# Row maximum of causal attention on TensorE: one head per bank and step, against three heads in three banks per burst on 32-row groups

## What is computed

```
q = (h @ Wq.T) as 16 heads of 32;  k = h @ Wk.T;  v = h @ Wv.T   (one key and value head for all 16)
q, k = rmsnorm(rope(q)), rmsnorm(rope(k))
scores = q k^T * 32**-0.5, causal
attn = softmax(scores);  out = attn @ v
x = x + ga * (rmsnorm(out) @ Wo.T)
then: layer norm, router (8 of 64 experts), experts and a shared MLP, x = x + gb * ffn
```

## Time and profile before

| | us |
|---|---|
| median of three runs | 1232.77 (1232.52 to 1236.47) |
| span of the profiled execution | 1233.0 |
| PE busy in it (matmul) | 1168.1 (95%) |
| VectorE busy | 972.6 (79%) |
| ScalarE busy | 762.0 (62%) |
| row maximum matmuls (L1092), 384 | 146.7 |
| row maximum reductions (L1610), 304 | 191.3 |

### The profile page before, as it was taken

How to read it: one execution, slowest core, us unless ns; L and a number is a source line. 1 busy time by engine, 2 the same in 40 slices (tenths; PEclk the granted TensorE clock), 3 DMA queues, 4 the chain that set the end, 5 groups by cost and what they waited for, 6 DMA issues and landing times.

```text
span 1233.0 us, 25541 instructions
## 1 busy us (share of the span) xinstructions
PE 1168.1 (95%) x8905; PEld 879.7 (71%) x8905; DVE 972.6 (79%) x1881; ACT 762.0 (62%) x1507; POOL 497.9 (40%) x375
## 2 busy tenths in 40 slices
PE   8988999999999988999999999999999999999996
PEld 4455556555565655555557899999999999999982
DVE  4678776756657888775767889899888999999976
ACT  3456555555664644455564477787777887777841
POOL 1122212102122111201100148887888778788740
PEclk9999999989999998999999999999999999999999
DMA  9570000000000000003004179999999999999988
GB/s 349 172 302 1 2 18 2 10 9 2 15 10 10 9 1 22 1 10 95 29 14 141 25 225 299 289 302 302 292 295 306 299 297 296 298 301 294 298 231 290
DMA packets 75167, 189.95 MB, mean 154 GB/s; under 512 B 11544, under 2 KB 12184, under 8 KB 74832
## 3 DMA queue, kind: packets, MB, share of 16 engines
q1 hardware_dynamic: 44704, 116.27, 28.0%
q0 software_dynamic: 28672, 71.32, 23.5%
q10 hardware_dynamic: 1712, 1.32, 0.3%
HBM read 136.36 MB, written 52.51 MB: 153 GB/s over the span
## 4 chain that ended last, share of the span: by engine, by line
PE 71%; DVE 13%; DVEq 4%; issue 3%; DMA 3%; ACT 3%; POOL 0%; SPq 0%; POOLq 0%; ACTq 0%
PE ps L1328 22%; PE ps L1367 12%; PE ps L1147 8%; PE ps L1314 5%; PE ps L1177 4%; PE ps L1132 4%; PE ps L1060 4%; PE ps L1092 4%; DVE nmax L1610 3%; PE ps L1117 2%; DMA acc_dram<-y,slots 1%; PE ps L1032 1%; PE ps L1164 1%; DMA wq<-in_wq_t 1%; PE ps L1195 1%
## 5 line engine op out<-in xcount | busy, mean ns | idle before, releaser
L730 POOL DMA_INDIRECT acc_dram<-y,slots x128 | 252.2, 1971 | 74.1 <-issue 47.9
L1610 DVE TENSOR_REDUCE nmax<-ps 128x1 f32<-128x512 f32 (+3 forms) x304 | 191.3, 656 | 95.3 <-PE ps L1096 52.4
L839 ACT ACTIVATE probs<-ps 128x512 f32<-128x512 f32 (+1 forms) x320 | 159.0, 554 | 87.2 <-PE ps L1132 86.3
L681 POOL TENSOR_SCALAR_AFFINE_SELECT probs<-probs 128x512 f32<-128x512 f32 x64 | 44.3, 691 | 376.7 <-ACT probs L839 376.6
L715 POOL DMA_INDIRECT xg<-h_dram,slots x128 | 130.7, 1021 | 84.4 <-DVE slots L1801 40.5
L1092 PE MATMUL ps<-kpad,qpT 128*128 128x512 f32 (+3 forms) x384 | 146.7, 450 | 15.5 <-DVE nmax L1610 13.4
L1328 PE MATMUL ps<-x_hi,e_gu_hi 128*112 128x256 f32 (+1 forms) x768 | 120.1, 278 | 0.0
L1132 PE MATMUL ps<-qT,kT 98*128 98x512 f32 (+1 forms) x320 | 115.1, 437 | 5.0 <-ACT probs L839 4.8
L1328 PE MATMUL ps<-x_hi,e_gu_lo 128*112 128x256 f32 (+1 forms) x768 | 119.6, 278 | 0.0
L1812 DVE TENSOR_TENSOR e_gu_lo<-e_gu,e_gu_hi 128x1408 fp32r<-128x1408 f32 x64 | 103.8, 1622 | 11.0 <-ACT e_gu_hi L960 9.9
L1328 PE MATMUL ps<-x_lo,e_gu_hi 128*112 128x256 f32 (+1 forms) x768 | 109.9, 279 | 0.0
(11 more groups left out here) (238 smaller groups left out, 2375.1 us busy)
## 6 DMA issues: line engine op xcount, KB each, us to landing
e_gu<-in_gate_up SPq DMA_DIRECT2D x64, 704.0 KB, 7.3
e_d<-in_w_down SPq DMA_DIRECT2D x64, 224.0 KB, 4.7
acc_dram<-h SPq DMA_DIRECT2D x2, 4608.0 KB, 26.0
e_d<-in_w_down SPq DMA_DIRECT2D x64, 128.0 KB, 5.4
wmod_b<-in_wmod SPq DMA_DIRECT2D x2, 2048.0 KB, 22.0
xg<-h_dram SPq DMA_DIRECT2D x16, 256.0 KB, 7.0
acc_a<-acc_dram SPq DMA_DIRECT2D x8, 512.0 KB, 10.0
acc_b<-acc_dram SPq DMA_DIRECT2D x8, 512.0 KB, 7.7
```

The lines of the kernel that those rows point to most:

```text
L730: pool.indirect_dma_start(out=acc_dram[a], out_offset=bass.IndirectOffsetOnAxis(ap=slots[:, at:at + 1], axis=0), in_=y[e % 2][:, h, :], in ...
L839: act.activation(probs[:, n % PROBS, 2 * pr:2 * pr + 2, off:CW], unit_bank(2 * n + pr)[:, :, off:CW], ACT.Exp).then_inc(s_exp, 1)
L1610: dve.tensor_reduce(nmax[:, 1 if lo else 0, first:first + heads], max_view(n, heads, hi - lo), AX.X, ALU.max, negate=True).then_inc(s_max, 1)
```

## The change

The keys are stored without zeros: `kq` holds the same 32 rows of keys on all four groups of 32 partitions. For that DVE writes the keys four times side by side (`ks4`), PE transposes them once more to 128 rows, and ACT copies them once. A head's matmul then reads only its own 32 rows of `qpT` and `kq`. The banks of a tile are ordered so that banks next to each other hold heads of different row groups. Up to three banks make a burst: PE issues the matmuls of its banks in turn, one of each bank, then the mask matmuls; DVE takes the maximum over all banks of the burst with one instruction (two where the widths differ). A tile has 2, 3, 6, 6, 7, 8, 11, 11 bursts by its place i, spread over the 16 steps, 108 in all. The three banks are the same as before, so PE waits before each burst until the one before it is reduced. The pass still has 384 matmuls and 176 mask matmuls, and 116 reductions. The memset of `kpad` is gone.

```diff
--- before.py
+++ after.py
-        kpad = sb(att, "kpad", [P, GH, S], f32r)
+        kq = sb(att, "kq", [P, S], f32r)
+        ks4 = sb(att, "ks4", [P, GH, HD])
...
+        def max_parts(i):
+            width = (i + 1) * P
+            return [(lo, min(width, lo + 512)) for lo in range(0, width, 512)]
+        def max_banks(i):
+            found = []
+            for part, (lo, hi) in enumerate(max_parts(i)):
+                k = heads_in(hi - lo)
+                for n in range(H // k):
+                    q, j = divmod(n, GH)
+                    found.append((part * H + n * k, [GH * (q * k + a) + j for a in range(k)], lo, hi))
+            return found
+        def bursts(i):
+            banks = max_banks(i)
+            return [banks[n:n + MAX_BANKS] for n in range(0, len(banks), MAX_BANKS)]
+        def bursts_at(i, h):
+            found = bursts(i)
+            return [(n, banks) for n, banks in enumerate(found) if n * H // len(found) == h]
...
@@ keys_out (ACT)
-                for j in range(GH):
-                    r = slice(HD * j, HD * j + HD)
-                    last = act.activation(kpad[r, j, i * P:i * P + P], ps[0:HD, T_BANK, 0:P], ACT.Copy)
+                last = act.activation(kq[:, i * P:i * P + P], ps[:, T_BANK, P:2 * P], ACT.Copy)
...
@@ pack_keys (PE)
-                pe.transpose(ps[0:QK, T_BANK, 0:P], ks[:, :], ident).then_inc(s_pack_k, 1)
+                pe.transpose(ps[0:QK, T_BANK, 0:P], ks[:, :], ident)
+                pe.transpose(ps[:, T_BANK, P:2 * P], ks4[:, :, :].rearrange("p j d -> p (j d)"), ident)\
+                  .then_inc(s_pack_k, 1)
...
@@ row_max (PE)
-                    if n >= MAX_BANKS:
-                        pe.wait_ge(s_max, n - MAX_BANKS + 1)
-                    for a in range(heads):
-                        last = pe.matmul(view[:, a, :], qpT[:, t % 2, (first + a) // GH, :],
-                                         kpad[:, (first + a) % GH, lo:hi], start=(a == 0),
+                    if bursts_before(t) + n:
+                        pe.wait_ge(s_max, bursts_before(t) + n)
+                    for a in range(max(len(heads) for _, heads, _, _ in banks)):
+                        for k, (_, heads, lo, hi) in enumerate(banks):
+                            if a < len(heads):
+                                g, j = divmod(heads[a], GH)
+                                r = slice(HD * j, HD * j + HD)
+                                last = pe.matmul(max_view(k, 1, hi - lo)[:, a, :], qpT[r, t % 2, g, :], kq[r, lo:hi],
...
@@ start and split (DVE)
-            dve.memset(kpad[:, :, :].bitcast(f32), 0.0)
+                    dve.tensor_copy(ks4[:, :, :].bitcast(f32r), t1[:, H, :].unsqueeze(1).to_broadcast([P, GH, HD]))
...
@@ row_max (DVE)
+                for n, banks in bursts_at(i, h):
+                    dve.wait_ge(s_mm, bursts_before(t) + n + 1)
+                    while k < len(banks):
+                        last = dve.tensor_reduce(nmax[:, first:first + alike * len(heads)], max_view(k, alike, hi - lo), AX.X, ALU.max,
+                                                 negate=True)
+                        k += alike
+                    last.then_inc(s_max, 1)
```

More of the change, by code:

```diff
@@ L804, in pack_out @@
                 if t >= 2:
-                    act.wait_ge(s_mm, pieces_before(t - 1))
+                    act.wait_ge(s_mm, bursts_before(t - 1))
                 act.activation(qpT[:, t % 2, :, :], ps[:, T_BANK, :].rearrange("p (g t) -> p g t", t=P), ACT.Copy)\
@@ L813, in keys_out @@
                 if t and i == 0:
-                    act.wait_ge(s_mm, pieces_before(t))
-                for j in range(GH):
-                    r = slice(HD * j, HD * j + HD)
-                    last = act.activation(kpad[r, j, i * P:i * P + P], ps[0:HD, T_BANK, 0:P], ACT.Copy)
+                    act.wait_ge(s_mm, bursts_before(t))
+                last = act.activation(kq[:, i * P:i * P + P], ps[:, T_BANK, P:2 * P], ACT.Copy)
                 last.then_inc(s_packT, 1)
@@ L1086, in row_max @@
                         pe.wait_ge(s_packT, t + 1)
-                    n += pieces_before(t)
-                    if n >= MAX_BANKS:
-                        pe.wait_ge(s_max, n - MAX_BANKS + 1)
-                    view, diagonal = max_view(n, heads, hi - lo), hi == (i + 1) * P
-                    for a in range(heads):
-                        last = pe.matmul(view[:, a, :], qpT[:, t % 2, (first + a) // GH, :],
-                                         kpad[:, (first + a) % GH, lo:hi], start=(a == 0),
-                                         stop=(a == heads - 1 and not diagonal))
-                    if diagonal:
-                        last = pe.matmul(view[:, :, hi - lo - P:hi - lo], ident_b[:, :],
-                                         bias_b[:, :].unsqueeze(1).to_broadcast([P, heads, P]), start=False, stop=True)
+                    if bursts_before(t) + n:
[6 more added lines that the diff above has]
+                                last = pe.matmul(max_view(k, 1, hi - lo)[:, a, :], qpT[r, t % 2, g, :], kq[r, lo:hi],
+                                                 start=(a == 0), stop=(a == len(heads) - 1 and hi != (i + 1) * P))
+                    for k, (_, heads, lo, hi) in enumerate(banks):
+                        if hi == (i + 1) * P:
+                            last = pe.matmul(max_view(k, 1, hi - lo)[:, :, hi - lo - P:hi - lo], ident_b[:, :],
+                                             bias_b[:, :].unsqueeze(1).to_broadcast([P, len(heads), P]), start=False, stop=True)
                     last.then_inc(s_mm, 1)
```

56 lines of the change are left out of this document (24 added, 32 removed).

## The result

The changed kernel takes 1239.1 us in the median (1238.76 to 1242.35, 7 runs), against 1232.5 us of the kernel before on the same chip. The ratio, taken of the means, is 1.0062, with a 95% interval of 1.0043 to 1.0081: slower by 0.6%, where the prediction had 1218, faster by 1.2%. The profiled execution took 1240.6 us from first to last instruction; that of before 1233.0.

A forecast was written before the change was run, and what follows sets the result against it. PE was taken as the bound, with DVE close behind. The terms 15.6 - 9 + 3.4 + 3 + 3 - 1.5 = 14.5 us off 1233.0 gave a forecast of 1218 us, with 1202 to 1247 as the range for 8 in 10.

The forecast's parts named there:

- The near end of PE's work: Row maximum matmuls on PE: three banks in the time of one, 48 us instead of 74.5, 26.4 us less.
- Rivals 1 and 4: Row maximum on PE: 1, weight loads do not overlap, 1234 us, chance 0.20; 4, row groups never run together, 1248, 0.08.
- Times 0.59: Row maximum matmuls: share of their PE time on the path, turning 26.4 us less work into 15.6 us gained.
- The round trip: Between bursts, PE waits for DVE's whole reduction and DVE for PE's whole burst: 9 us lost, bounds 0 and 17.
- the 35 that the prediction named as harmless: Sign in the next profile: PE's waits for DVE's reductions about 35 us instead of 25.4; 60 or more means rival 2.
- rival 2: Row maximum: the round trip between PE and DVE becomes the bound, 35 us against gains of 23.5: 1245 us, chance 0.20.
- The granted clock: Side remark in rival 2: a PE with more pauses could lose more at 1.2 instead of 2.4 GHz; no size given.
- Its share of 0.18, 3.4 us: DVE's row maximum reductions: 188 fewer instructions save 19 us of work, at the path's share 0.18 a 3.4 us gain.
- `end_max`, 3 us: End of each tile's row maximum: the last reduction comes earlier, so PE need not wait; 3 us gained (0 to 8).
- Keys, 1.5 us net: Key storage: 3 us gained from PE's waits for `kpad`, 1.5 us lost to added transposes and DVE copies.

The follow-up runs named there:

- e3: Changed kernel with 128-row matmuls against the four zero-padded key copies instead of row groups, bursts and single reduction kept: 1252.4 us, ratio 1.0175.
- e4: Changed kernel with two dummy matmuls of 512 columns ahead of each burst, behind its wait: 1268.1 us, ratio 1.0308.
- e5: Changed kernel with one extra unused 384-column maximum on DVE per burst, behind the signal that frees the banks to PE: 1260.5 us, ratio 1.0229.
- e6: Changed kernel with one extra unused 384-column maximum on DVE per burst, ahead of the signal that frees the banks to PE: 1278.1 us, ratio 1.0366.
- e14: Changed kernel with bursts placed on half steps, 1.5 steps apart for i = 6 and 7: 1230.8 us, ratio 1.0003.
- e2: Changed kernel with DVE reducing bank by bank and PE waiting for each bank alone, bursts and row groups kept: 1247.1 us, ratio 1.0129.
- e11: Changed kernel with the keys stored as before, in four zero-padded copies, bursts and row groups kept: 1248.6 us, ratio 1.0144.
- e17: Changed kernel with bursts on half steps, as e14, but without any dummy matmuls in the stacking: 1234.3 us, ratio 1.0014.

## Why the prediction was wrong

**The near end of PE's work: right.** Three matmuls in the time of one, next work after 0.43 us, loads within 0.01 us of each other. Rivals 1 and 4 are out. 108 bursts at that pace are 46 us of PE, where 48 were forecast.

**"Times 0.59": 15.6 us forecast, and about that arrived, in part by luck.** Row groups and new keys were to give 15.6 + 3 - 1.5 = 17 us; e3 and the changed kernel give 14 as measured, 18 at like clock. But the relief was put too low: the row of two matmuls in 0.50 us holds one of 512 and one of 384 columns, so 0.25 us for 512 was too little. e3 has 0.27, and its 108 bursts, each from its first load to the next work on PE, add up to some 80 us at 2.4 GHz, where the prediction had 74.5; those of the changed kernel add up to 48. So over 30 us went instead of 26.4, and about half of it reached the time. A share of the path is no law: at the head of a burst e4 has 0.63, or 0.8 at like clock.

**The round trip, "bounds 0 and 17 us; I take 9": the mechanism right, the size wrong.** This is the first step that failed. Only pairs one step apart were counted, and only by what they fall short of 2.5 us. The terms that belong to the bursts were -9 + 3.4 + 3 = -2.6 us; e3 measured -22, some -16 at like clock. PE's waits for DVE rose by 23 us, from 38.8 to 61.9. The 37.6 us of its weight loads are close to the 35 that the prediction named as harmless; the other 24.3 stand with the matmuls, in a row that it didn't read. DVE's own waits rose by 11 us, and its path by 11. e5 and e6 show that the release counts, and e14 that close bursts do. This is rival 2, at 1239 instead of 1245. The Trainium skill, "TensorEngine Tiling (Array Packing)", section PSUM Bottleneck, says that tiling speeds up TensorE and not the emptying of PSUM, and the trace agrees: a burst is 0.43 us of PE and 1.76 us of DVE.

**The granted clock: left out of the sum.** This is the second step that failed. It stood as half a sentence in rival 2, without a price. 31 us more at 1.2 GHz at 0.27 to 0.35 us each are 8 to 11 us, more than the whole loss of 7.6 us between the profiled executions. At like clock the changed kernel would be 1 to 3 us ahead of before. So of the 22 us between forecast and result (14.5 gained against 7.6 lost) some 10 are the clock, and some 12 the bursts' round trip; this split is an estimate. The two are not independent: when the round trip grew with nothing else on PE (e5, e6), so did the time at 1.2 GHz.

**DVE**: 1.755 us for 1536 columns (1.77 forecast) and 20.4 us less work (19). Its share of 0.18, 3.4 us, was probably too small: e2 has the instructions back and is 8 us slower (5 at like clock), with 23 us less waiting on PE.

**`end_max`, 3 us**: the wait went from 8.2 to 1.8, but `qT` came 6.5 us later on PE's loads, so nothing arrived there. **Keys, 1.5 us net**: about right at like clock. e11 shows a loss of 10 us without the new keys by the ratios, but its executions have 26 us more at 1.2 GHz than the changed kernel's, worth 8. Why the clock falls with the old keys, perhaps by the four copies in front of the first burst, was not tested.

What stays open: why the clock falls in one execution and not in another of the same instructions, as in tile 4. e14 to e17 vary by 14 to 17 us from run to run, the kernel before by 7, and dummy work did not narrow this.

## What to carry to other kernels

Where a change merges buffers that took turns into one that is filled and emptied as a whole, cost the round trip for every use, and not only for the closest pairs (9 us were put here, and bursts alone cost 22), and spread the uses evenly (7 us here, by half a step) before anything else. Where the granted clock already falls, a lighter TensorE may pay part of its gain back: put that in the sum, here at 0.3 us for each us at 1.2 GHz. And compare times and clocks of the same executions: one profiled execution need not have the clock of the median.

## What the runs showed of the hardware

- A visit to 32-row groups takes 0.43 us until the next 128-row matmul, with one bank or with three in different groups; three matmuls of 512 columns on 128 rows take 0.80 us (e3), 0.27 each.
- Weight loads of 128 columns for different row groups run side by side: three in 0.19 us, where four on the whole array take 0.53, 0.113 us apart.
- The maximum of 512, 1024 and 1536 columns takes 0.69, 1.22 and 1.755 us on DVE: 0.53 for each 512 and 0.16 once.
- Of the same instructions in tile 4, one execution had the clock at 2.4 GHz throughout and another 17 us at 1.2 GHz: 26.9 against 32.9 us.
